# One-head attention in a four-layer kernel: fp16 passes for scores and values, the softmax scaling on GpSimd, turns two tiles behind the scores

## What is computed

```
q = x @ Wq + bq
k = x @ Wk + bk
v = x @ Wv + bv
scores = einsum('bqh,bkh->bqk', q, k) / sqrt(128)
attn = softmax(scores, axis=-1)
a = einsum('bqk,bkh->bqh', attn, v) @ Wo + bo
x = x + a
```

## Time and profile before

| | before |
|---|---|
| median of 3 runs | 4643.16 us (4641.54 to 4646.2) |
| the profiled execution | 4609.9 us |
| its span, first to last instruction | 4607.5 us |
| instructions | 88670 |
| TensorE's granted clock, mean | 0.947 of full speed |

### The profile page before, as it was taken

How to read it: one execution, slowest core, us unless ns; L and a number is a source line. 1 busy time by engine, 2 the same in 40 slices (tenths; PEclk the granted TensorE clock), 3 DMA queues, 4 the chain that set the end, 5 groups by cost and what they waited for, 6 DMA issues and landing times. The chain is left out here.

```text
span 4607.5 us, 88670 instructions
## 1 busy us (share of the span) xinstructions
PE 4042.7 (88%) x34700; PEld 2257.5 (49%) x34700; DVE 3472.0 (75%) x4781; ACT 2982.6 (65%) x4498; POOL 2365.3 (51%) x1443
## 2 busy tenths in 40 slices
PE   5999999999998989985877777896888869999998
PEld 2666666666676644441111211344777443444443
DVE  5888888888884557756889898574777747888888
ACT  2777777777775459952677777782665726555564
POOL 2888888888884013320221110461666526666665
PEclk7999999999999989985899999897999979999999
DMA  2122212221120011100120100340000333333342
GB/s 81 45 51 57 57 42 51 57 57 48 48 48 1 1 70 46 69 1 28 62 73 31 43 22 13 109 138 26 13 14 13 102 92 94 95 100 99 95 105 75
DMA packets 139405, 261.47 MB, mean 57 GB/s; under 512 B 23908, under 2 KB 71908, under 8 KB 137388
## 3 DMA queue, kind: packets, MB, share of 16 engines
q1 hardware_dynamic: 123572, 215.01, 17.2%
q0 software_dynamic: 15424, 40.89, 2.6%
HBM read 170.31 MB, written 49.76 MB: 48 GB/s over the span
## 5 line engine op out<-in xcount | busy, mean ns | idle before, releaser
L513 POOL TENSOR_TENSOR a_prob_low<-a_prob_whole,a_prob_high 128x1024 f16<-128x1024 f32 x512 | 1084.9, 2130 | 276.6 <-ACT a_prob_high L403 276.6
L487 DVE TENSOR_REDUCE a_part_max<-a_top 128x2 f32<-128x1024 f32 x512 | 626.1, 1223 | 218.6 <-PE a_top L314 212.6
L400 ACT ACTIVATE a_prob_whole<-a_score 128x1024 f32<-128x1024 f32 x512 | 525.3, 1026 | 332.4 <-PE a_score L303 320.4
L757 ACT ACTIVATE a_prob<-a_score 128x512 f32<-128x512 f32 x1024 | 533.0, 603 | 260.7 <-PE a_score L701 260.7
L789 DVE TENSOR_REDUCE a_part_max<-a_side 128x2 f32<-128x1024 f32 x512 | 595.1, 1219 | 86.3 <-PE a_side L672 86.3
L1920 POOL TENSOR_TENSOR m_scaled<-m_acted,m_gate 128x512 f32<-128x512 f32 x264 | 433.2, 1649 | 271.5 <-DVE m_acted L2038 201.6
L403 ACT ACTIVATE a_prob_high<-a_score 128x1024 f16<-128x1024 f32 x512 | 521.9, 1019 | 0.0
L302 PE MATMUL a_score<-a_qa,a_ka 128*128 128x256 f16 x2048 | 476.2, 273 | 0.0
L303 PE MATMUL a_score<-a_qb,a_kb 128*128 128x256 f16 x2048 | 476.1, 273 | 0.0
L369 PE MATMUL a_o_ps<-a_v,a_prob_high 128*128 128x65 f16 x4096 | 428.1, 193 | 6.3 <-POOL a_prob_low L513 3.4
L371 PE MATMUL a_o_ps<-a_v,a_prob_high 128*128 128x64 f16 x4096 | 426.9, 194 | 0.0
(11 more groups left out here) (440 smaller groups left out, 10378.0 us busy)
## 6 DMA issues: line engine op xcount, KB each, us to landing
m_gate<-gates SPq DMA_DIRECT2D x264, 256.0 KB, 5.1
a_ka<-a_nat_high_k SPq DMA_DIRECT2D x128, 128.0 KB, 2.4
e_gate<-gates SPq DMA_DIRECT2D x8, 2048.0 KB, 7.0
slots<-in_slots SPq DMA_DIRECT2D x19, 520.0 KB, 4.1
a_qa<-a_nat_high_q SPq DMA_DIRECT2D x64, 128.0 KB, 2.4
a_qa<-a_nat_low_q SPq DMA_DIRECT2D x64, 128.0 KB, 2.4
a_qb<-a_nat_high_q SPq DMA_DIRECT2D x64, 128.0 KB, 2.4
a_kb<-a_nat_low_k SPq DMA_DIRECT2D x64, 128.0 KB, 2.4
```

Source lines behind the costliest of these rows:

```text
L400: eng.activation(prob_whole[:, e % RING, :, :, :], score[:, e % 2, :, :, :], ACT.Exp, scale=scale)
L487: eng.tensor_reduce(part_max[:, i, c, :, qt % 4], top[:, :, :], AX.X, ALU.max).then_inc(max_done, 1)
L513: eng.tensor_tensor(prob_low[:, e % RING, :, :, :], prob_whole[:, e % RING, :, :, :], prob_high[:, e % RING, :, :, :], ALU.subtract).then_ ...
L757: eng.activation(prob[:, e % RING, h, :], score[:, step % SLOTS, :], ACT.Exp).then_inc(exp_done, 1)
```

## The change

Scores and values are computed from fp16 pairs. Each operand x is split into x_high = fp16(x) and x_low = fp16(x - x_high), and a product becomes three fp16 matmuls: high x high, high x low, low x high. For k and q, ACT makes the high part in an operation of its own behind the bias and POOL the low part. For v and the turned prob, ACT's copy out of PSUM writes the high part and DVE's subtraction from PSUM the low part, in two halves of 512 columns each; `turned` becomes two half buffers. The turn of a tile comes two steps behind its scores instead of one. Values are computed for four tiles at once (moving operand of 512 columns) in the four steps that begin six steps behind the first tile's scores, two of eight key tiles per step. DVE keeps the reciprocal, now behind the maximum of the next tile, and POOL multiplies prob by it. POOL's stream follows `order` too, so its splits, multiplies and residual adds have a fixed order. The core of the diff:

```diff
-        for s in range(tiles + 3):
+        for s in range(tiles + 7):
             b, t = s // qts, s % qts
             if s < tiles:
                 order.append(("scores", s))
-            if 1 <= s < tiles + 1:
-                order.append(("turn", s - 1))
+            if 6 <= s < tiles + 6:
+                order.append(("values", s - 6))
             if 2 <= s < tiles + 2:
-                order.append(("values", s - 2))
+                order.append(("turn", s - 2))
             if b + 1 < B and t in (4, 5, 6):
                 order.append(("kqv"[t - 4], b + 1))
-            if s >= 3 and (s - 3) % 4 == 3:
-                order.append(("proj", (s - 3) // 4))
+            if s >= 10 and (s - 10) % 4 == 0:
+                order.append(("proj", (s - 10) // 4))
...
+        prob_high = pl.sb("prob_high", [P, 2, qts, BANK], F16)
+        prob_low = pl.sb("prob_low", [P, 2, qts, BANK], F16)
         mixed = pl.sb("mixed", [P, 2, BANK])
         wide_ps = pl.ps("wide", [P, 2, N])
-        turned = pl.ps("turned", [P, N])
+        turned = pl.ps("turned", [P, 2, HALF, P])
...
+                def product(dst, highs, lows, first, last):
+                    eng.matmul(dst, highs[0], highs[1], start=first, stop=False)
+                    eng.matmul(dst, highs[0], lows[1], start=False, stop=False)
+                    return eng.matmul(dst, lows[0], highs[1], start=False, stop=last)
...
-                    elif what == "v":
-                        if turn[job]:
-                            eng.wait_ge(turned_read, turn[job])
-                        for t in range(qts):
-                            mm = eng.matmul(turned[:, t * P:(t + 1) * P], xn_t[:, n * N + t * P:n * N + (t + 1) * P], w[:, 2, :],
-                                            start=True, stop=True)
-                        mm.then_inc(turned_full, 1)
+                    elif what in ("v", "turn"):
+                        if what == "turn":
+                            eng.wait_ge(prob_ready, n + 1)
+                        for h in range(2):
+                            i = turn[what, n, h]
+                            if i >= 2:
+                                eng.wait_ge(turned_read, i - 1)
+                            for t in range(HALF):
+                                kt = h * HALF + t
+                                if what == "v":
+                                    mm = eng.matmul(turned[:, h, t, :], xn_t[:, n * N + kt * P:n * N + (kt + 1) * P], w[:, 2, :], start=True, stop=True)
+                                else:
+                                    mm = eng.transpose(turned[:, h, t, :], prob[:, n % 3, kt * P:(kt + 1) * P], ident[:, :])
+                            mm.then_inc(turned_full, 1)
                     elif what == "scores":
                         if t == 0:
-                            wait_freed(eng, ("k", b))
-                            wait_freed(eng, ("q", b))
+                            eng.wait_ge(qk_split, 2 * (b + 1))
+                        here = slice(t * P, (t + 1) * P)
                         for h in range(2):
-                            mm = eng.matmul(dst[:, h * BANK:(h + 1) * BANK], q[:, b % 2, t * P:(t + 1) * P],
-                                            k[:, b % 2, h * BANK:(h + 1) * BANK], start=True, stop=True)
+                            at = slice(h * BANK, (h + 1) * BANK)
+                            mm = product(dst[:, at], (q_high[:, b % 2, here], k_high[:, b % 2, at]), (q_low[:, b % 2, here], k_low[:, b % 2, at]), True, True)
                         mm.then_inc(wide_full, 1)
-                    elif what == "turn":
-                        eng.wait_ge(prob_ready, n + 1)
-                        eng.wait_ge(turned_read, turn[job])
-                        for kt in range(qts):
-                            mm = eng.transpose(turned[:, kt * P:(kt + 1) * P], prob[:, n % 3, kt * P:(kt + 1) * P], ident[:, :])
-                        mm.then_inc(turned_full, 1)
                     elif what == "values":
-                        eng.wait_ge(turned_read, turn["turn", n] + 1)
-                        if n % 4 == 0 and n:
-                            eng.wait_ge(mixed_half, n // 4)
-                        for kt in range(qts):
-                            mm = eng.matmul(mix[:, t % 4 * P:(t % 4 + 1) * P], v[:, b % 2, kt, :], prob_t[:, n % 2, kt * P:(kt + 1) * P],
-                                            start=(kt == 0), stop=(kt == qts - 1))
-                        mm.then_inc(mixed_tile, 1)
+                        m, i = n // 4, n % 4
+                        if i == 0:
+                            eng.wait_ge(turned_read, turn["turn", 4 * m + 3, 1] + 1)
+                            if m:
+                                eng.wait_ge(mixed_half, m)
+                        for kt in (2 * i, 2 * i + 1):
+                            mm = product(mix[:, :], (v_high[:, b % 2, kt, :], prob_high[:, m % 2, kt, :]),
+                                         (v_low[:, b % 2, kt, :], prob_low[:, m % 2, kt, :]), kt == 0, kt == qts - 1)
+                        mm.then_inc(mixed_part, 1)
...
-                for job in by_act:
+                for job in order:
                     what, n = job
                     if what == "k":
                         eng.wait_ge(wide_full, slot[job] + 1)
-                        eng.activation(k[:, n % 2, :], wide_ps[:, slot[job] % 2, :], ACT.Identity, bias=bias[:, 1:2]).then_inc(act_freed, 1)
+                        if n:
+                            eng.wait_ge(qk_split, 2 * n - 1)
+                        eng.activation(k[:, :], wide_ps[:, slot[job] % 2, :], ACT.Identity, bias=bias[:, 1:2]).then_inc(act_freed, 1)
+                        wait_freed(eng, job)
+                        eng.activation(k_high[:, n % 2, :], k[:, :], ACT.Copy).then_inc(qk_high_done, 1)
+                    elif what == "q":
+                        wait_freed(eng, job)
+                        eng.activation(q_high[:, n % 2, :], q[:, :], ACT.Copy).then_inc(qk_high_done, 1)
                     elif what == "scores":
                         eng.wait_ge(negated, n + 1)
                         if n >= 3:
-                            eng.wait_ge(turned_full, turn["turn", n - 3] + 1)
+                            eng.wait_ge(turned_full, turn["turn", n - 3, 1] + 1)
                         eng.activation(prob[:, n % 3, :], wide_ps[:, slot[job] % 2, :], ACT.Exp, bias=top[:, n % 4:n % 4 + 1],
                                        accum_out=total[:, n % 4:n % 4 + 1]).then_inc(act_freed, 1)
-                    elif what == "v":
-                        eng.wait_ge(turned_full, turn[job] + 1)
-                        if n >= 2:
-                            eng.wait_ge(mixed_tile, qts * (n - 1))
-                        eng.activation(v[:, n % 2, :, :].rearrange("p a b -> p (a b)"), turned[:, :], ACT.Copy).then_inc(turned_read, 1)
-                    elif what == "turn":
-                        eng.wait_ge(turned_full, turn[job] + 1)
-                        if n >= 2:
-                            eng.wait_ge(mixed_tile, n - 1)
-                        eng.activation(prob_t[:, n % 2, :], turned[:, :], ACT.Copy).then_inc(turned_read, 1)
+                    elif what in ("v", "turn"):
+                        if what == "v" and n >= 2:
+                            eng.wait_ge(mixed_part, qts * (n - 1))
+                        if what == "turn" and n >= 8:
+                            eng.wait_ge(mixed_part, 4 * (n // 4 - 1))
+                        for h in range(2):
+                            eng.wait_ge(turned_full, turn[what, n, h] + 1)
+                            eng.activation(parts_of(what, n, h)[0], turned[:, h, :, :], ACT.Copy).then_inc(turned_high, 1)
...
-                def normalise(n):
+                def invert(n):
                     wait_freed(eng, ("scores", n))
                     eng.reciprocal(total[:, n % 4:n % 4 + 1], total[:, n % 4:n % 4 + 1]).then_inc(inverted, 1)
-                    eng.wait_ge(inverted, n + 1)
-                    eng.tensor_scalar(prob[:, n % 3, :], prob[:, n % 3, :], total[:, n % 4:n % 4 + 1], None, ALU.mult).then_inc(prob_ready, 1)
 
                 for job in order:
                     what, n = job
                     if what == "q":
                         eng.wait_ge(wide_full, slot[job] + 1)
-                        eng.tensor_scalar(q[:, n % 2, :], wide_ps[:, slot[job] % 2, :], bias[:, 0:1], scale, ALU.add, ALU.mult).then_inc(dve_freed, 1)
+                        if n:
+                            eng.wait_ge(qk_split, 2 * n)
+                        eng.tensor_scalar(q[:, :], wide_ps[:, slot[job] % 2, :], bias[:, 0:1], scale, ALU.add, ALU.mult).then_inc(dve_freed, 1)
                     elif what == "scores":
-                        if n:
-                            normalise(n - 1)
                         eng.wait_ge(wide_full, slot[job] + 1)
                         at = slice(n % 4, n % 4 + 1)
```

(38 more changed lines are left out.)

24 lines of the change are left out of this document (19 added, 5 removed).

## The result

The changed kernel takes **4695.23 us** (median of 4 runs, 4692.06 to 4701.65), beside 4642.35 us of the kernel before on the same chip: ratio 1.012 [1.0106, 1.0134], 52.9 us slower. The forecast was 4659, 16 slower, with a range that ended at 4676: the sign held, the size did not. The profiled execution took 4692.06 us.

The account below looks back on a forecast made before the run. PE was taken to bound the kernel before, a DVE-ACT round the changed one. Start +2.6, loop -4.5 and end +6.2 gave +4.3; with +12 for the clock, +16: 4659 us, range 4642 to 4676.

Parts of the forecast that it names:

- The round between DVE and ACT: Plain tiles: maximum, negation, exp, ACT's copy and low-part subtractions run in series, 4.40 us per tile against 5.48.
- the step with `xp_t`: Every fourth tile, `xp_t` on DVE stands between low part and maximum and adds 0.67 us.
- the batch changes: Three times, POOL's splits of k and q stand ahead of multiplies due sooner; each batch pays about 10 us.
- PE's load: Fewer, cheaper fp16 records for scores and values: PE loses 1.0 us per tile, 32 in all.
- The start: First scores wait until the splits of k and q are done, q's deciding; first maximum +2.6 us.
- the clock's term: Half clock for 3.4 us behind seven PE holes: 10.2 us at batch changes, 1.7 at the end, +12 together.
- the end: Behind the last maximum, multiply, turn, copies, values and projection take 18.7 us instead of 12.4: +6.2.
- I take 1.04, because this has one tensor input too.: Length in us of POOL's multiply by the reciprocal, between bounds of 1.04 (cast) and 2.36 (two-input product).
- All cost nothing in a plain step: Added waits of PE's values, DVE's maximum and ACT's exp cost 0 in plain steps, but are late at batch changes.
- Clock holds: Rival: PE's holes leave the clock at 1.00; only +4.3, 4647 us, chance 0.20.
- the holes vanish: Rival: POOL's multiplies at batch changes come in time, each batch takes 13.9 us; 4617 us, chance 0.07.
- POOL slow: Rival: POOL's multiply takes 2.36 us, +9 on the forecast, 4668 us; chance 0.10.

Follow-up runs that it names:

- seventh: Changed kernel with six residual adds on POOL each issued behind the next multiply: 4680.1 us, ratio 1.0067.
- eleventh: Changed kernel with both the splits and the residual adds later in POOL's order, multiply still on POOL as changed: 4598.3 us, ratio 0.9981.
- the second experiment: Changed kernel with the splits of the next batch's k and q issued later in POOL's order, nothing else moved: 4619.08 us, ratio 1.0027.
- fourth: Changed kernel with POOL's multiply written as a tensor-by-tensor product with the reciprocal broadcast along the row: 4643.85 us, ratio 1.0078.
- sixth: Changed kernel with short extra matmuls (256 columns, result unread) ahead of each turn to keep PE busy: 4680.3 us, ratio 1.007.
- the first: Changed kernel with the multiply back on DVE behind the reciprocal, POOL keeping only splits and residual adds: 4602.73 us, ratio 0.9991.
- the tenth: Changed kernel with the multiply on DVE plus lines meant to reorder POOL's jobs, which left POOL's order unchanged: 4605.75 us, ratio 0.9996.

## Why the prediction was wrong in size

**Right, with its size.** The round between DVE and ACT: 4.40 predicted, 4.37 measured in every kernel whose plain tiles were not bounded by a filler; the step with `xp_t` was given 0.67 more and takes 5.02, 0.65 more, in three of the four steps outside the batch changes in the seventh and eleventh, and 6.35 in the fourth, of which more below. PE's load: 32 us less predicted for 32 tiles, 29 measured in the loop once the clock is nearly full (156.9 to 127.9). The start: +2.6 predicted, +3.1 measured; first scores wait for the split of q. (The prediction counts eight long multiplies beside POOL's add before; the trace has seven. No term uses it.) The multiply in a plain tile costs nothing, even at 2.84: it has 5 us. That the change ends slower, and that it does so because POOL's order puts splits ahead of due multiplies: the second experiment moved these six instructions alone and got 38.6 us.

**Where the 37 us beyond the forecast lie.** 17.7 in the steps outside the batch changes (112.5 for 94.8), 15.8 in the batch changes (96.7 for 70.7, of which the clock's term had 10.2), 3.4 at the end (+11.3 for +6.2 and 1.7 of clock), 0.5 at the start.

**The step that failed first: "I take 1.04, because this has one tensor input too."** The multiply took 2.84, outside both ends. The bounds came from a cast and from a two-input product, and neither was a multiply by a scalar; that none of the rows showed this operation was said, and yet both ends were taken from operations with another form. The rule cited there from the Trainium skill (GPSIMD Engine Reference, section 4.1 Engine selection), that POOL is roughly at line rate for one input, does not hold for this operation: 2.84 us on POOL against 0.75 on DVE, 3.8 times. By its price for two inputs the sum would have been nearer, for no reason that the runs bear out. Six exposures of 1.8 us in the batch changes alone would be 10.8 us of the 26 by which these outgrew the forecast at full clock. The runs say that it costs more than its exposure: 0.95 us less (fourth) took 7.8 us from them, where six exposures are 5.7, and keeping PE busy (sixth) took 7.4. How the 26 divide between length and clock is not shown, since a longer multiply also makes a longer hole.

**The step that was missing: the residual add on POOL.** The list of POOL's order at the batch change was written down, but not the one behind a projection, where the add waits for `xp_t` ahead of a multiply that is ready. It costs 17.5 us (seventh experiment), and with it goes nearly all of the excess of the steps outside the batch changes: 112.5 us measured, 94.8 forecast, 96.3 in the seventh. The two missed steps work together: with the adds where they were and the multiply at 1.89 (fourth) these steps take 104.2, so about half of this cost hangs on the length of the multiply behind the add. "All cost nothing in a plain step" named PE's, DVE's and ACT's queues and left out POOL's.

**The step that was too small: +12 for the clock.** The mechanism was right: the holes shown above are followed by half clock. But the forecast had seven falls of 3.4 us, six in the loop and one at the end. Read in windows of half a microsecond, the stage after has fifteen stretches at half clock (of which one, at its start, is there before as well), 72 us together, five of those in the batch changes 6.5 to 10 us long. Six of them go with the place of the residual adds, for the seventh has nine, and the batch changes' holes were 6.6 and 4.9 us where the forecast had 3.9 and 3.2. Nor do the rows bear out a fall in every hole, or in none of the plain ones: the first two holes of the earlier trace rows are equally long (PE idle for 2.94 and 2.93 us), and half clock followed only one; the half clock at 3912.7 followed 3.29 us, a hole that the rows do not show. In the eleventh PE waited 2.02 us at 1579.46, as it does in every plain step, and the turn behind it took 1.92 us, half clock; that made the step with `xp_t` 6.35 us instead of 5.02:

```profile
1579.46 0.39 PE L953 MATMUL b_mix<-b_prob_high,b_v_high 128*128 128x512 f16 x1 [2.02 <-DVE b_prob_low L1067]
...
1580.79 1.92 PE L981 MATMUL b_turned<-all_kept_ident,b_prob 128*128 128x128 f32 x8
```

The changed kernel has two such steps, the first has two and the tenth, the same program, none, which is most of the 3 us between them. Keeping PE busy gave back 14.1 us of the loop (sixth), and the matmuls of the loop are 22.2 us longer than at a clock of 0.97.

**The end, +11.3 for +6.2.** With the multiply on DVE it was 20.8 us, +7.0 to the 13.8 of before; so the term's own working was right to 0.8 us. With the multiply on POOL and the adds late (seventh, eleventh) it is 22.1, so 3.0 of the rest is the sixth add's place in POOL's order, and 1.3 the multiply with what clock it costs.

**The rivals.** "Clock holds" and "the holes vanish" are out: the clock was 0.85 and the turn behind k_low waited 6.6 us. "POOL slow" was the right rival with 0.10, and even its price, 2.36, was too low; taken at 2.84 it would still have missed the add. "The holes vanish" had the right place, POOL's work at the batch change, and the eleventh kernel is nearly what it described: not because POOL caught up, but because the splits moved out of its way. Its three batch changes take 54.9 us where that rival had 41.7.

## What to carry to other kernels

When an operation moves to an engine that serves in order, write that engine's whole queue down, at every kind of step, and ask of each instruction what ready work stands behind its wait; here the order alone was worth 58 us and the length of the moved operation, once the order was right, nothing that could be measured beside the 3 us by which loops of one program differed. And bound an operation that the trace lacks only by rows of the same form of instruction on that engine. Where there is none, leave the price open above the dearest row: "one input" said nothing about its rate, and 2.84 us lay above every row that served as a bound. Last, check that an edit to a queue's order still moves an instruction on that engine; the tenth kernel's did not.

## What the runs showed of the hardware

POOL's rates for 128x1024 fp32: cast 1.04 us, product with a broadcast column 1.89, multiply by a scalar 2.77 (constant) to 2.84 (column). On this engine the form with two tensor operands was the faster way to scale a row.

DVE's multiply took 0.75 us alone and 2.59 when it started 0.08 us behind a POOL subtraction of 2.13 us. The Trainium skill (SBUF — State Buffer, section "Who interferes with whom") says that DVE in a two-port mode and POOL contend, and that whoever issues first holds the shared ports for its whole instruction while the other is blocked. No row names the mode of this multiply, but the times agree: 2.59 is the 2.05 us that POOL still had to run and 0.54 more.

PE's clock fell behind waits of 2.0 to 6.6 us and, behind others of 2.0 and of 2.9, did not.
